# A mixture-of-experts stage with two raw buffers for the down weights, gathered two groups ahead

## What is computed

```python
shared = (silu(x @ sh_gate_w.T) * (x @ sh_up_w.T)) @ sh_down_w.T      # 1408 wide
top_v, top_i = top_k(softmax(x @ router_weight.T), 2)                 # 8 experts, 2 of them for each token
for e in range(8):
    gate, up = split(x @ gate_up_proj[e].T)                           # 352 wide each
    out += (silu(gate) * up) @ down_proj[e].T * combine[:, e:e + 1]
out += sigmoid(x @ shared_gate_w.T) * shared
```

## Time and profile before

| | before |
|---|---|
| time, median of 3 runs | 2009.27 us (2005.46 to 2009.52) |
| the profiled execution: span | 2000.4 us |
| matmuls, weight loads busy | 1895.7, 1536.0 us |
| DVE, ACT, POOL busy | 1083.5, 844.6, 439.6 us |

### The profile page before, as it was taken

How to read it: one execution, slowest core, us unless ns; L and a number is a source line. 1 busy time by engine, 2 the same in 40 slices (tenths; PEclk the granted TensorE clock), 3 DMA queues, 4 the chain that set the end, 5 groups by cost and what they waited for, 6 DMA issues and landing times.

```text
span 2000.4 us, 27565 instructions
## 1 busy us (share of the span) xinstructions
PE 1895.7 (95%) x9880; PEld 1536.0 (77%) x9880; DVE 1083.5 (54%) x2590; ACT 844.6 (42%) x1718; POOL 439.6 (22%) x438
## 2 busy tenths in 40 slices
PE   7789999999999998999999999999999999999997
PEld 5567777777777776777777778778989888998875
DVE  4556665554554553464464454433656666666566
ACT  4334443333343332333344233123556656656554
POOL 2301001001001001001000100121455555555322
PEclk9889999999999998999999999999999999999998
DMA  8978566557367356446546456786788888888597
GB/s 304 373 258 310 184 246 250 198 187 258 122 234 259 126 173 243 177 163 239 205 174 224 171 181 240 243 325 236 236 253 241 247 247 240 255 250 251 130 283 198
DMA packets 140869, 456.84 MB, mean 228 GB/s; under 512 B 17200, under 2 KB 17344, under 8 KB 123968
## 3 DMA queue, kind: packets, MB, share of 16 engines
q1 hardware_dynamic: 90720, 251.70, 35.7%
q0 software_dynamic: 49584, 203.33, 33.0%
q10 hardware_dynamic: 432, 0.07, 0.0%
HBM read 332.99 MB, written 122.04 MB: 227 GB/s over the span
## 4 chain that ended last, share of the span: by engine, by line
PE 56%; DMA 5%; DVE 5%; ACT 2%; issue 1%; POOL 1%; SPq 1%; ACTq 0%; DVEq 0%
PE banks L796 16%; PE banks L798 16%; PE banks L797 16%; DMA moe_dn_raw<-w_dn,w_index 3%; PE banks L863 2%; PE banks L989 1%; DMA ffn_w_raw<-w_ffn 1%; PE banks L877 1%; PE banks L995 1%; PE banks L883 1%; PE banks L870 1%; DMA att_w_lo<-att_w_split 1%; PE banks L829 1%; ACT moe_dn_hi L1134 0%; DVE fin_stats L1535 0%
## 5 line engine op out<-in xcount | busy, mean ns | idle before, releaser
L796 PE MATMUL banks<-xT_hi,ffn_gate_up_hi_lo 128*128 128x512 f32 x704 | 296.7, 422 | 9.8 <-DMA xT_lo<-xt_scratch 3.3
L798 PE MATMUL banks<-xT_hi,ffn_gate_up_hi_lo 128*128 128x512 f32 x704 | 276.8, 393 | 0.0
L797 PE MATMUL banks<-xT_lo,ffn_gate_up_hi_lo 128*128 128x512 f32 x704 | 276.1, 392 | 0.0
L796 PE MATMUL banks<-moe_gu_hi,moe_xT_hi 128*128 128x352 f32 x568 | 196.5, 346 | 4.2 <-DVE moe_xT_lo L1515 4.1
L1067 ACT COPY q_one_head<-qT 32x128 f32<-32x128 f32 x512 | 151.2, 295 | 89.5 <-PE banks L863 84.0
L1508 DVE TENSOR_TENSOR moe_gu_lo<-moe_gu_raw,moe_gu_hi 128x704 fp32r<-128x704 f32 x156 | 136.0, 889 | 90.4 <-ACT moe_gu_hi L1128 85.7
L798 PE MATMUL banks<-moe_gu_hi,moe_xT_lo 128*128 128x352 f32 x568 | 183.4, 323 | 0.0
L797 PE MATMUL banks<-moe_gu_lo,moe_xT_hi 128*128 128x352 f32 x568 | 182.6, 321 | 0.0
L796 PEld LDWEIGHTS banks<-xT_hi,ffn_gate_up_hi_lo 128*128 128x128 f32 x704 | 133.1, 189 | 49.2 <-issue 10.2
L797 PEld LDWEIGHTS banks<-xT_lo,ffn_gate_up_hi_lo 128*128 128x128 f32 x704 | 133.2, 189 | 33.9 <-issue 8.9
L798 PEld LDWEIGHTS banks<-xT_hi,ffn_gate_up_hi_lo 128*128 128x128 f32 x704 | 132.9, 189 | 29.0
(11 more groups left out here) (315 smaller groups left out, 4157.6 us busy)
## 6 DMA issues: line engine op xcount, KB each, us to landing
ffn_gate_up_hi_lo<-ffn_gate_up_split SPq DMA_DIRECT2D x66, 1024.0 KB, 4.8
ffn_down_hi_lo<-ffn_down_split SPq DMA_DIRECT2D x66, 512.0 KB, 3.4
att_w_hi<-att_w_split SPq DMA_DIRECT2D x112, 256.0 KB, 4.0
att_w_lo<-att_w_split SPq DMA_DIRECT2D x112, 256.0 KB, 4.8
x_normed_by_expert<-x_normed POOLq DMA_DIRECT2D x26, 771.0 KB, 16.1
ffn_w_raw<-w_ffn SPq DMA_DIRECT2D x44, 384.0 KB, 6.0
ffn_gate_up_split<-ffn_gate_up_hi_lo SPq DMA_DIRECT2D x11, 1024.0 KB, 4.0
x_in<-x SPq DMA_DIRECT2D x32, 256.0 KB, 4.8
```

The lines of the kernel that those rows point to most:

```text
L796: pe.matmul(out_ap, l_hi, r_hi, start=start, stop=False)
L797: pe.matmul(out_ap, l_hi, r_lo, start=False, stop=False)
L798: return pe.matmul(out_ap, l_lo, r_hi, start=False, stop=stop)
```

## The change

The raw down weights get a second buffer, at the end of the tiles of the expert stage, and a semaphore for each buffer. Group g uses buffer g % 2. The gather that stands behind the last down cut of group g is now that of group g + 2, and it waits for the cuts of group g, as the one before it did. The gather of group 1 moves into the burst of gathers in the shared FFN, behind `rgu` 1, and that of group 2 takes its old place.

```diff
-            if kind == "WD" and n == DT - 1 and g + 1 < NG:
-                out.append(("rdn", g + 1))
+            if kind == "WD" and n == DT - 1 and g + 2 < NG:
+                out.append(("rdn", g + 2))
...
-            parts[1] += [("rgu", 0), ("rdn", 0), ("xg", 0), ("xg", 1), ("xg", 2), ("rgu", 1)]
+            parts[1] += [("rgu", 0), ("rdn", 0), ("xg", 0), ("xg", 1), ("xg", 2), ("rgu", 1), ("rdn", 1)]
...
-            parts[2] += [("rdn", 1)]
+            parts[2] += [("rdn", 2)]
...
-        rdn = sb("moe_dn_raw", [DT * D], scope=phase2)
+        rdn_first = sb("moe_dn_raw", [DT * D], scope=phase2)
...
+        rdn = [rdn_first, sb("moe_dn_raw_other", [DT * D], scope=phase2)]
...
-        rdn_in = sem("moe_dn_in")
+        rdn_in = [sem(f"moe_dn_in{i}") for i in range(2)]
...
-                if g:
-                    pool.wait_ge(v_piece, done("V", "WD", g - 1, DT - 1))
+                if g >= 2:
+                    pool.wait_ge(v_piece, done("V", "WD", g - 2, DT - 1))
                 pool.indirect_dma_start(
-                    out=rdn[:, :], out_offset=None, in_=wdn_d[:, :],
-                    in_offset=bass.IndirectOffsetOnAxis(ap=widx[:, g:g + 1], axis=0)).then_inc(rdn_in, 16)
+                    out=rdn[g % 2][:, :], out_offset=None, in_=wdn_d[:, :],
+                    in_offset=bass.IndirectOffsetOnAxis(ap=widx[:, g:g + 1], axis=0)).then_inc(rdn_in[g % 2], 16)
...
-                act.wait_ge(rdn_in, 16 * (i + 1))
+                act.wait_ge(rdn_in[i % 2], 16 * (i // 2 + 1))
...
-                op = act.copy(dn_hi[:, i % 2, k, :], rdn[:, k * D:(k + 1) * D])
+                op = act.copy(dn_hi[:, i % 2, k, :], rdn[i % 2][:, k * D:(k + 1) * D])
...
-                op = ve.tensor_tensor(dn_lo[:, i % 2, k, :], rdn[:, k * D:(k + 1) * D], dn_hi[:, i % 2, k, :].bitcast(F32),
+                op = ve.tensor_tensor(dn_lo[:, i % 2, k, :], rdn[i % 2][:, k * D:(k + 1) * D], dn_hi[:, i % 2, k, :].bitcast(F32),
```

## The result

| | before | after |
|---|---|---|
| time, median of the runs | 2009.39 us (2005.46 to 2009.97, 4 runs) | 1979.65 us (1978.43 to 1980.47, 4 runs) |
| the profiled execution: span | 2000.4 us | 1977.9 us |
| matmuls, weight loads busy | 1895.7, 1536.0 us | 1883.4, 1530.1 us |

The ratio of after to before is 0.9857, with a 95% interval of 0.9843 to 0.9871. The kernel is faster by 29.7 us where 24.4 had been forecast.

A forecast was written before the change was run, and what follows sets the result against it. TensorE was taken to set the pace, stalled by late down gathers: -20.9 (gaps) - 4.6 (low clock) + 1.1 (small stalls) + 0 = -24.4 us. Forecast 1984.9 us; own range 1980.5 to 1990, 8-in-10 range 1980.5 to 1995.

The forecast's parts named there:

- The account of the stage: Expert stage: late down gathers cost TensorE 25.5 us; the pace of 68 moe_y evictions gave 25.6 us.
- 20.9 us of gaps and 4.6 us of low clock: Expert stage: TensorE weight-load waits from late down gathers, plus 1.2 GHz running after the three longest; both should go.
- The 1.1 us for small stalls: Expert stage: 1.1 us kept for small stalls of other causes, bounds 0 and 4 us.
- The early gather of group 1: Shared FFN: moving this gather into the burst was taken to cost 0; upper bound 0.4 us exposed plus 1.5 low clock.
- The sign that the stages ahead keep their length to 1 or 2 us: Profile after: stages before 1392 us, and after the last expert, should keep their lengths to 1 or 2 us.
- the distance between the median and the profile: Whole kernel: the median stood 8.9 us above the profiled span, and this distance was kept after the change.
- The distance of 15 us after the change: Expert stage: some 15 us left from a down gather's issue to its copy, against landings up to 9.2 us.
- Rival A: Expert stage: scatter-adds waiting for earlier adds hold the first groups, bringing back 4.0 us of stalls: 1988.9 us, chance 0.10.
- C: Expert stage: the loop of adds paces the whole stage and loses once landings exceed 8.1 us: 2022 us, chance 0.05.
- B: Expert stage: moe_hT or another copy is late in the same steps; half of 25.5 us stays: 1996.5 us, chance 0.07.
- D: Expert stage: gathers stay late or another limit fills the stalls: 2009 us, within 0.2%, chance 0.05.
- E: Expert stage: ACT's waits for down gathers are worth their full 41.1 us: 1968 us, chance 0.02.

The follow-up runs named there:

- before_again: The kernel before, unchanged, profiled a second time: 2013.7 us, with a span of 2011.9 us.
- one_ahead: The kernel after with its two buffers, but each down gather only one group ahead, at its old place in POOL's queue: 2002.7 us, ratio 0.999 to before.
- slot_later: The kernel after with each down gather issued one step later, at the end of the next step, still two groups ahead: 2012.4 us, ratio 1.0015 to before.
- slot_half: The kernel after with each down gather at the head of the next step, behind its add and row gather, ahead of the gate/up gather: 1995.3 us, ratio 0.992.
- late_first: The kernel after with the gather of group 1 moved out of the shared FFN's burst, directly ahead of that of group 2: 1978.5 us, ratio 0.987 to before.
- after_again: The kernel after, unchanged, run and profiled again as a reference: 1979.8 us, ratio 0.987 to before.
- gather_once: The kernel before with its single buffer, issuing only group 0's down gather; all groups use those weights: 1983.4 us, ratio 0.986 to before.
- y_two: The kernel after with two buffers of moe_y in place of four: 1977.1 us, ratio 0.985 to before.
- y_three: The kernel after with three buffers of moe_y in place of four: 1977.3 us, ratio 0.986 to before.

## Why the prediction was right, and where it was off
**The account of the stage holds.** 20.9 us of gaps and 4.6 us of low clock had been summed to 25.5 us, and the evictions gave the same a second way; the stage became 25.4 us shorter. The low clock is a part of it: the five profiles with down gathers late, set against the floor of 456.5 us, close with it to 0.9 us, always from above, and without it four of them miss by 4 to 12 us.

| profile | 68 steps | above the floor | gaps | time at 1.2 GHz | gaps + half of it |
|---|---|---|---|---|---|
| before | 481.9 | 25.4 | 20.9 | 9.9 in 3 | 25.9 |
| before_again | 488.9 | 32.4 | 26.3 | 13.7 in 4 | 33.1 |
| one_ahead | 483.6 | 27.1 | 21.1 | 13.7 in 4 | 27.9 |
| slot_later | 493.0 | 36.5 | 24.8 | 25.3 in 6 | 37.5 |
| slot_half | 466.6 | 10.1 | 9.3 | 2.5 in 1 | 10.6 |
| late_first | 457.0 | 0.5 | 0.6 | 0 | 0.6 |
| after, after_again, gather_once, y_two, y_three | 456.5 | 0 | 0 | 0 | 0 |

(All in us; gaps of weight loads over 0.25 us between the first and the 69th eviction; time of granted clock 0.50 outside these gaps.) The Trainium skill (Perfetto Trace Analysis, Identifying the Most-Contended Engine) asks for the busy share of the weight loads, beside the share of the peak arithmetic rate, to see how near TensorE is to its peak; the prediction took the gaps in front of the weight loads instead. By the share, 438.5 of 493.0 us leaves 54.5 us free, yet after the change 32.2 of 468.0 us are still without a weight load while matmuls fill 467.7: the share doesn't say what this change could win. Matmuls left 16.8 us free, the gaps were 20.9, and 25.4 us came. The gaps are the nearest, and still short by the clock.

**The 1.1 us for small stalls** was not needed in the profile after: no new gap came in the stage. late_first had one of 0.56 us, so 1.1 is a fair bound and 0 the usual value.

**The early gather of group 1, taken at 0, bounds 0 and 1.9.** Four of the six profiles with it show no cost. The gap of 1.8 us in the profile after may be its price, but gather_once has one of 1.1 us without it, so no run shows the price. My reason was wrong in any case: I wrote that only the gathers get longer by it. The load of the shared weights got longer too, and about 0.3 us are left of its slack in y_three (10.1 of 10.4). The sign that the stages ahead keep their length to 1 or 2 us didn't come in the profile after, whose expert stage began 3.3 us later, 1.8 of them by that gap.

**The term that was wrong is the distance between the median and the profile.** I kept the 8.9 us between span and median as if they lay around the span, because the page gives no time for it, and subtracted the same gain from both. 1.8 us lie around the span. The other 7.1 us are what the median run took longer than the profiled one. No profile of a run at the median was taken, so where they lie is not shown directly; but before_again has 7.0 us more in the stage, and in the four groups of runs the median of before stands 26.7 to 29.7 us above those of the kernels without such stalls (after, after_again, late_first, y_two, y_three, gather_once), between the 25.4 and 32.4 us that the stage lost in the two profiles. Most of the 7.1 us were stalls, then, and the change removes these as well: 24.4 + 7.1 = 31.5 us would have been the forecast against the median, and 29.7 us came. The spread of the runs before, 4 us, was no clear hint: 2.0 us after the change against 4.5 in these runs and 3.0 against 14.6 in the next, but late_first, y_two, y_three and gather_once, with hardly a stall in their profiles either, spread by 5.2 to 6.9 us in 4 runs each.

**The distance of 15 us after the change** was too hopeful. I took the issue times of before and moved the use. In the profile after, POOL was late: the shortest distances from issue to use were 10.4 and 10.6 us. They were 12.9 us in after_again and 7.4 in late_first. In the profile after, one gather and the first copy from it:

```profile
1477.19 0.94 POOL L669 DMA_INDIRECT moe_dn_raw<-w_dn,w_index  x1 [0.30 <-DVE moe_gu_lo L1509]
...
1488.37 0.63 ACT L1135 CAST moe_dn_hi<-moe_dn_raw 128x512 fp32r<-128x512 f32 x1
```

11.2 us, still without a wait.

**Rival A's mechanism was there, without its price.** Adds waited for earlier adds for 40.6 us in the profile after and 27.6 in after_again, where it was 19.0 before. How late that makes POOL differs from one execution to the next: an add started up to 7.9 us behind the end of its eviction in after, 5.9 in after_again and 10.6 in late_first, against 6.3 and 6.8 in the two profiles of before. The adds' landing rose from 5.6 us in the median (5.9 in before_again) to 7.0, though by only 0.5 us in each of its two kinds, as told at the end:

```profile
L683 POOL DMA_INDIRECT ffn_out<-moe_y,moe_x x68: 1552/1622/2341, 1411.0 to 1855.5; - x68
...
DMA to landing us min/median/max: 4.7/7.0/9.1
```

(after_again; the first profile of after has no landing times.) In the first groups the loop was 1451.63 - 1438.12 = 13.5 us long there, at two steps of 6.71 us just too long to catch up, and not the 14.1 of the earlier trace rows. TensorE noticed none of it in after, after_again, y_two and y_three; the 0.56 us of late_first came with the largest lag.

**C** put two ways of counting side by side: 8.06 us of landing counted from the end of the add on POOL, and 5.6 and 8.6 us that the profile counts from its start. The add of 1441.04 landed 8.9 us after its start, in a loop of 14.1. So the loop would lose from a landing of 8.9 us on, which 3 of 68 adds passed in after_again and 12 in late_first, and at 8.6 us, the landing that C took, it would not have been slower than before. **B** fell: no copy was late in the steps of the profile after, and in late_first copies waited for a gate/up gather, 0.96 us at most. **D** and **E** fell: 25.4 us of 41.1 came in the stage.

## What to carry to other kernels
A second buffer does nothing by itself; it pays by the lead that it allows, so look at the time from a transfer's issue to its first use against its landing, and at what is issued directly in front of it. Where an in-order engine waits for a transfer, price the gap that reaches TensorE, not the engine's own wait, add what the clock loses behind some of the gaps, and check against the pace of one repeated instruction. Before subtracting from a median, ask how far the profiled execution is from it: a kernel whose stalls vary from run to run loses more in its median than a lucky profile shows.

## What the runs showed of the hardware that I had not expected
- Five profiles have 30 gaps of 1.5 us and more on TensorE's weight loads in these steps. 18 of them led into or ended in a stretch at 1.2 GHz (granted clock 0.50 and 0.51 in the windows), 12 didn't, and the length of the gap alone doesn't decide. A gap of 3.20 us in before_again was followed by full clock, one of 1.80 us in slot_later, with one of 0.31 us behind it, by half. Each gap, and the window behind it:

```profile
1564.33 0.19 PEld L796 LDWEIGHTS banks<-moe_dn_hi,moe_hT_hi 128*128 128x128 f32 x1 [3.20 <-DVE moe_hT_lo L1517]
1564.33:1567.60 3.27, 3.26 (x17) 2.83 (x18) 1.58 (x3) 1.41 (x4) 0.94 (x1) 1.00 0.89 365
...
1748.58 0.19 PEld L799 LDWEIGHTS banks<-moe_gu_hi,moe_xT_hi 128*128 128x128 f32 x1 [1.80 <-DVE moe_xT_lo L1518]
1750.30:1753.60 3.30, 3.30 (x10) 2.42 (x9) 1.50 (x2) 0.14 (x1) 2.06 (x2) 0.50 1.04 293
```

- A down gather of 0.79 MB landed in 6.8 to 7.8 us in the median in the seven profiles in which most stood directly behind a row gather of 0.26 MB, and in 9.1 us in slot_later, where 35 of 36 stood directly behind a gate/up gather of 1.44 MB on the same queue. Inside after_again it was 7.1 us for the first kind and 9.1 us for the second.
- A load on SyncE's queue felt one more gather on POOL's queue: the landing of the second of the two gate/up loads went from 8.8 to 9.0 us, in four profiles, to 9.4 to 10.1 us, in four others.
- The adds come in two kinds. From before to after_again the median landing of the 30 second pieces of a group went from 7.0 to 7.5 us, that of the 38 first pieces from 5.0 to 5.5; the median of all 68 went from 5.6 to 7.0 because it moved from one kind to the other. In gather_once, without 38 of the down gathers, only the landings of the second pieces could be read, 7.0 us in the median, as in before (7.2 in before_again). So the down gathers don't make these adds slow; what added the 0.5 us after the change stays open.
